# Expert rows of a mixture-of-experts kernel: loaded in 32x32 blocks and transposed by VectorE instead of TensorE

## Chip, cores and metric

One Trainium2 chip, 1 core. The metric is the device time of the whole program in microseconds (us); the median of three runs before the change is 1184.05 us.

## What is computed

The input x is (4, 1024, 256) in float32. The first layer adds to x the layernorm of a state-space mixer of layernorm(x). The second, which the change touches, adds the layernorm of a mixture of experts:

```python
xn = (xf - mu) * rsqrt(var + LN_EPS) * ln_gamma + ln_beta      # 4096 tokens x 256
topv, topi = top_k(softmax(xn @ router_w), 2)                   # 8 experts, 2 a token
for e in range(E):
    out = out + comb[:, e:e+1] * _swiglu(xn, gate_up_w[e], down_w[e])   # F = 1024
out = out + _swiglu(xn, shared_gate_up_w, shared_down_w)
```

_swiglu is silu(clip(gate)) * up @ down. All is done to float32 accuracy: each operand is split into a high and a low part, and a product is three matmuls (high x high, high x low, low x high).

## The kernel before

**Mixer stage** (to about 465 us of the profile). Four batches pass through the mixer, and each engine follows a list of stages written out by hand (ORDER, one string for each engine). Beside it, the experts' weights are split into high and low parts: SyncE loads chunk after chunk (`n0` to `n15` of each batch; `load_raw`, L385), ScalarE rounds it (L776) and VectorE subtracts (L1014), SyncE stores the two halves (L397, L398). A slot of the ring of three is loaded again once its stores have landed. Tokens are normalised (without gamma and beta), routed, and scattered by GpSimd (L1150) into `xs_scratch`, one row of ROW = 260 floats each: 256 values and four that hold token, expert code and shares. The shared expert runs there too.

**Expert stage** (488 to 1135 us, and its first group from 465 us). The rows lie sorted by expert and are taken in NG = 39 groups of G = 256 rows; a group belongs to one expert. The groups of the expert with most rows come first (`star`), so that its rows and weights can be loaded ahead: SyncE's stages `rw` (`first_rows`, L1253 to L1256, groups 0 and 1) and `ww` (`first_weights`). Each engine then runs `turn(g)` over the FC = 8 chunks f of the hidden width:

- TensorE: `gate_up(g, f)` is 12 matmuls (L1354 to L1356), `down` 6 (L1365 to L1367), LAG = 3 chunks behind, so that a turn's first three downs are the group before's chunks 5 to 7. After `gate_up` 1 and 4 it transposes one 128-column half c of the next group's rows into PSUM (`turn_rows`, L1342: two 128x128 transposes against `ident`).
- VectorE: clip of the gate (L1464), low part of the chunk before (`h_low`, L1459), product with the up part (L1471); after chunk 2 `weigh`, after 3 and 6 `rows_lo` (L1437), after 3 `copy_y` (L1443).
- ScalarE: `h_high` (L1406), silu (L1414), and after chunks 2 and 5 `rows_hi`: two activations with gamma and beta from the transposed rows in PSUM (L1397, L1400).
- SyncE: for each f, once `down` of the group before has used the chunk's buffers, two weight loads (L1239 the gate-up part, 512 KB; L1240 the down part, 256 KB) under a condition: they move data only where the expert changes, and `gate_up(g, f)` waits for both. After chunk 1 comes `load_rows(g+1)` (L1226, L1227): a register load of the row number, and one DMA of 256 x 1040 bytes. Before it SyncE waits for the last transposes (`x_turned`) and for `weigh`. `others` begins with group 2's rows (its first issue of L1227) and then walks the turns.
- GpSimd: two indirect DMAs a group that add the outputs to `acc_scratch` (L1304).

`gate_up(f)` needs VectorE's product of chunk f-2 (the semaphore `h_ready` starts at 2). Weights, rows and hidden parts live in parts of the mixer's buffers ("homes"); down parts 0 to 5 lie in one buffer behind the gate-up parts, except part 1, which lies in `h_hi[0]`; parts 6 and 7 lie behind a gate-up part in `xs_hi` and `xs_lo`, part 6 at offset 0 behind it. A last stage (1135 us on) normalises and adds x.

```python
if c == 0:
    pe.wait_ge(rows_loaded[par], (g_half(g, par)) * 16 + 16)
pe.wait_ge(x_f_ready, g * DC + c + 1)
for t in range(GT):
    i = nc.tensor.transpose(x_ps[:, t * P:(t + 1) * P], rows[:, par, t, c * P:(c + 1) * P], ident[:, :])
```

Of the kernel before, what the change touches and what calls it, by code (L numbers as in the profile page):

```python
# [6 lines left out]
I32 = mybir.dt.int32  # L7
ALU = mybir.AluOpType
# [48 lines left out]
X_AT, D_AT, R_AT = 48, 48, 0  # L57
GUW = 2 * 4 * P
XS = 5


def mixer(nc, x, w_e, w_s, weights, full, consts, shared, xs_dram, x1_dram, acc_dram, fill, vec, ident,
# [3 lines left out]
    with ExitStack() as ctx:  # L66
# [157 lines left out]
        homes = (gu_ring, d_ring, quad(u_flat[:, R_AT:R_AT + 2 * GT * ROW]), quad(x_home[0]), quad(x_home[1]),  # L224
                 u_flat[:, R_AT + 2 * GT * ROW:R_AT + 2 * GT * ROW + DC * G].rearrange("p (c g) -> p c g", g=G),
                 cv_flat[:, 0:4 * G].rearrange("p (i g) -> p i g", g=G),
                 h_home[0].rearrange("p (i g) -> p i g", g=G), h_home[1].rearrange("p (i g) -> p i g", g=G),
# [35 lines left out]
        def used(k):  # L263
# [195 lines left out]
        def _(pe):  # L459
            first_turn, all_groups = e_tensor(pe)  # L460
# [159 lines left out]
            def sh_down(k, f):  # L620
# [3 lines left out]
                for t in range(2):  # L624
                    toks = slice((2 * f + t) * P, (2 * f + t + 1) * P)
                    for c in range(SC):
# [5 lines left out]
                           "g": sh_gate, "y": sh_down, "x": first_turn})  # L632
# [162 lines left out]
        def _(dve):  # L795
            seeds, first_lo, all_groups = e_vector(dve)
# [254 lines left out]
            run("vector", {"x": first_lo, "star": fullest, "m": x_moments, "p": split_low, "k": bias_sum, "c": conv_sides, "r": xs_remainder, "dt": delta_unit, "da": da_unit,  # L1051
# [127 lines left out]
def experts(nc, ctx, w_s, xs_dram, acc_dram, x1_dram, out, group_expert, group_change, group_row, group_code, vec, ident, neg_half,  # L1179
# [9 lines left out]
    w_gu, w_d, rows, xg_hi, xg_lo, xg_f, gate, hg_hi, hg_lo, y, acc, x1, small = homes  # L1189
# [16 lines left out]
    gu_ps, down_ps, x_ps = banks[0:2], [banks[2:4], banks[4:6]], banks[6]  # L1206
    loaded = [sem(f"chunk_loaded{f}") for f in range(FC)]
    rows_loaded = [sem(f"x_rows_loaded{i}") for i in range(2)]
    x_turned, x_hi_ready, x_f_ready, x_lo_ready = sem("x_turned"), sem("x_hi_ready"), sem("x_f_ready"), sem("x_lo_ready")
# [3 lines left out]
    y_added = [sem(f"y_added{i}") for i in range(2)]  # L1213

# [9 lines left out]
    def sync(sp):  # L1224
        def load_rows(g, par):
            row = sp.value_load(group_row[0:1, bass.ds(g, 1)], min_val=0, max_val=SPARE)  # L1226
            sp.dma_start(rows[:, par, :, :], xs_dram[bass.ds(row, G), :].rearrange("(t p) d -> p t d", p=P)  # L1227
                         ).then_inc(rows_loaded[par], 16)
# [24 lines left out]
        def first_rows(b, par=0):  # L1253
            row = sp.value_load(star[0:1, 1 + par:2 + par], min_val=0, max_val=SPARE)
            sp.dma_start(rows[:, par, :, :], xs_dram[bass.ds(row, G), :].rearrange("(t p) d -> p t d", p=P)
                         ).then_inc(rows_loaded[par], 16)  # L1256
# [8 lines left out]
        def others():  # L1265
# [17 lines left out]
            for par in range(2):  # L1283
                sp.wait_ge(rows_loaded[par], 16 * (NG // 2 + 1))
# [48 lines left out]
    def tensor(pe):  # L1333
        def turn_rows(g, par, c):

            if c == 0:
                pe.wait_ge(rows_loaded[par], (g_half(g, par)) * 16 + 16)
                if isinstance(g, int) and g == 0:
                    free(pe, "x_ps")
            pe.wait_ge(x_f_ready, g * DC + c + 1)  # L1340
            for t in range(GT):
                i = nc.tensor.transpose(x_ps[:, t * P:(t + 1) * P], rows[:, par, t, c * P:(c + 1) * P], ident[:, :])  # L1342
            i.then_inc(x_turned, 1)

# [13 lines left out]
        def down(g, par, f):  # L1358
            pe.wait_ge(h_lo_ready, g * FC + f + 1)
            if f == 0:  # L1360
                pe.wait_ge(y_ready, g + 1)
            for t in range(GT):
                toks = slice(t * P, (t + 1) * P)
                out = down_ps[par][t][:, 0:D]
                nc.tensor.matmul(out, hg_hi[:, f % 4, toks], d_hi[f], start=f == 0, stop=False)  # L1365
                nc.tensor.matmul(out, hg_hi[:, f % 4, toks], d_lo[f], start=False, stop=False)  # L1366
                i = nc.tensor.matmul(out, hg_lo[:, f % 4, toks], d_hi[f], start=False, stop=f == FC - 1)  # L1367
# [24 lines left out]
        return first_turn, rest  # L1392

    def scalar(act):
        def rows_hi(g, par, c):
            act.wait_ge(x_turned, g * DC + c + 1)
            nc.scalar.activation(xg_hi[:, par, c, :], x_ps[:, 0:G], ACT.Identity,  # L1397
                                 bias=vec[:, V_BE + c:V_BE + c + 1],
                                 scale=vec[:, V_G + c:V_G + c + 1]).then_inc(x_hi_ready, 1)
            nc.scalar.activation(xg_f[:, c, :], x_ps[:, 0:G], ACT.Identity,  # L1400
# [3 lines left out]
        def h_high(g, f):  # L1404
            act.wait_ge(h_ready, g * FC + f + 1 + 2)
            nc.scalar.activation(hg_hi[:, f % 4, :], gate[:, f % 4, :], ACT.Copy).then_inc(h_hi_ready, 1)  # L1406
# [27 lines left out]
    def vector(dve):  # L1434
        def rows_lo(g, par, c):
# [146 lines left out]
```

## Time and profile before

| what | value |
|---|---|
| runs | 1182.93, 1184.05, 1185.82 us; median 1184.05 |
| the profiled execution's own time | 1178.42 us |
| its span | 1176.3 us |
| PE busy | 1082.7 us (92%) |
| DVE busy | 833.1 us (71%) |
| ACT busy | 655.2 us (56%) |
| POOL busy | 302.2 us (26%) |
| DMA moved | 191.72 MB, mean 163 GB/s |
| mean granted TensorE clock | 0.973 of 2.4 GHz |
| chain that ended last | PE 75%, DVE 8%, issue 4%, DMA 4%, POOL 3%, SyncE's queue 3%, ACT 3% |

Times are from the span's start. PE is TensorE (PEld its weight load), DVE VectorE, ACT ScalarE, POOL GpSimd, SP or SPq SyncE, whose issues count as its queue's. The span's times are of the one profiled execution, 0.5% below the median of the runs.

### The profile page before, as it was taken

Reading aid. Unit: us, or ns where it says so; the run is one execution under the profiler, and the core shown is the slowest. Engines: PE = TensorE matmul, PEld = TensorE weight load, DVE = VectorE, ACT = ScalarE, POOL = GpSimd, SP = SyncE. Lnnn points to the kernel's source line nnn. Section 1 sums busy time; section 2 is a strip of 40 time slices with the busy share of each in tenths; the row PEclk is TensorE's granted clock in tenths of the full one; section 3 lists DMA queues with packets and bytes.
Section 4 is the critical chain, followed back from the end, with each engine's and each line's share of the span. In section 5 each row is a group of like instructions: output and inputs, shape, how many; then the busy total and the mean of one; then the engine's idle time right before and its main releaser. Section 6 shows DMA issues by size and latency. Waiting matters only on the chain.

```text
span 1176.3 us, 24227 instructions
## 1 busy us (share of the span) xinstructions
PE 1082.7 (92%) x7492; PEld 961.2 (82%) x7492; DVE 833.1 (71%) x2113; ACT 655.2 (56%) x1325; POOL 302.2 (26%) x358
## 2 busy tenths in 40 slices
PE   4889999899979998899999999999999999999940
PEld 2665776677757666899999999999999999999940
DVE  5996899898877766566666666666666666666645
ACT  6778867778574364444544454544445444545425
POOL 1142032733441534012211221122122212211225
PEclk9999999999998999999999999999999999999985
DMA  8654776974663789523321236746922268212239
GB/s 304 208 213 172 251 231 210 318 240 145 223 229 140 247 284 320 195 59 64 72 56 35 36 86 210 222 130 192 379 67 36 60 208 250 36 19 35 36 81 222
DMA packets 122219, 191.72 MB, mean 163 GB/s; under 512 B 9792, under 2 KB 76864, under 8 KB 122176
## 3 DMA queue, kind: packets, MB, share of 16 engines
q1 hardware_dynamic: 105760, 170.38, 42.7%
q0 software_dynamic: 16416, 20.85, 10.5%
q8 instruction: 17, 0.28, 0.1%
q14 instruction: 26, 0.21, 0.1%
HBM read 295.62 MB, written 86.41 MB: 325 GB/s over the span
## 4 chain that ended last, share of the span: by engine, by line
PE 75%; DVE 8%; issue 4%; DMA 4%; POOL 3%; SPq 3%; ACT 3%; another core or an unknown queue 0%; ACTq 0%; DVEq 0%; POOLq 0%
PE bank L1354 11%; PE bank L1356 11%; PE bank L1355 11%; PE bank L470 10%; PE bank L1365 6%; PE bank L1367 6%; PE bank L1366 6%; PE bank L464 4%; PE bank L465 3%; PE bank L466 3%; POOL xs_scratch L1150 2%; PE bank L1342 1%; DMA w_both<-w_split 1%; DVE h L902 1%; DVE xr L1495 1%
## 5 line engine op out<-in xcount | busy, mean ns | idle before, releaser
L1304 POOL DMA_INDIRECT acc_scratch<-cv,ids x78 | 124.3, 1594 | 548.5 <-DVE cv L1443 508.4
L1464 DVE TENSOR_SCALAR cv<-bank 128x256 f32<-128x256 f32 x312 | 132.3, 424 | 185.3 <-PE bank L1356 185.3
L1354 PE MATMUL bank<-h_hi,w_both 128*128 128x256 f32 x936 | 260.3, 278 | 1.7 <-DVE cv L1471 1.2
L1355 PE MATMUL bank<-h_hi,w_both 128*128 128x256 f32 x936 | 259.6, 277 | 0.0
L1356 PE MATMUL bank<-h_hi,w_both 128*128 128x256 f32 x936 | 259.6, 277 | 0.0
L1414 ACT ACTIVATE cv<-cv 128x256 f32<-128x256 f32 x312 | 130.5, 418 | 225.5 <-DVE cv L1464 224.7
L1406 ACT ACTIVATE h_lo<-cv 128x256 fp32r<-128x256 f32 x312 | 130.0, 417 | 114.9 <-DVE cv L1471 113.4
L1354 PEld LDWEIGHTS bank<-h_hi,w_both 128*128 128x128 f32 x936 | 176.5, 189 | 3.1 <-issue 2.1
L1356 PEld LDWEIGHTS bank<-h_hi,w_both 128*128 128x128 f32 x936 | 176.4, 188 | 0.0
L1355 PEld LDWEIGHTS bank<-h_hi,w_both 128*128 128x128 f32 x936 | 176.4, 188 | 0.0
L1471 DVE TENSOR_TENSOR cv<-bank,cv 128x256 f32<-128x256 f32 x312 | 132.6, 425 | 47.6 <-ACT cv L1414 43.9
L1459 DVE TENSOR_TENSOR h_lo<-cv,h_lo 128x256 fp32r<-128x256 f32 x312 | 129.7, 416 | 0.8 <-ACT h_lo L1406 0.6
L464 PE MATMUL bank<-xs_hi,w_both 128*128 128x512 f32 x224 | 99.8, 445 | 22.3 <-DVE delta L852 9.1
L1365 PE MATMUL bank<-w_both,h_lo 128*128 128x256 f32 x390 | 107.7, 276 | 0.0
L1366 PE MATMUL bank<-w_both,h_lo 128*128 128x256 f32 x390 | 107.7, 276 | 0.0
L1367 PE MATMUL bank<-w_both,h_lo 128*128 128x256 f32 x390 | 107.7, 276 | 0.0
L466 PE MATMUL bank<-xs_hi,w_both 128*128 128x512 f32 x224 | 90.0, 402 | 0.0
L465 PE MATMUL bank<-xs_lo,w_both 128*128 128x512 f32 x224 | 89.8, 401 | 0.0
L1150 POOL DMA_INDIRECT xs_scratch<-n,slot_now x64 | 69.6, 1087 | 62.1 <-DVE slot_now L990 33.0
L464 PEld LDWEIGHTS bank<-xs_hi,w_both 128*128 128x128 f32 x224 | 43.9, 196 | 40.2 <-issue 14.6
L1133 POOL TENSOR_TENSOR h_lo<-h,h_hi 128x512 fp32r<-128x512 f32 x32 | 49.0, 1535 | 106.2 <-ACT h_hi L724 106.0
L1365 PEld LDWEIGHTS bank<-w_both,h_lo 128*128 128x128 f32 x390 | 73.2, 188 | 0.0
(233 smaller groups left out, 2558.2 us busy)
## 6 DMA issues: line engine op xcount, KB each, us to landing
w_both<-w_split SPq DMA_DIRECT2D x228, 512.0 KB
w_both<-w_split SPq DMA_DIRECT2D x190, 256.0 KB
e_raw<-w_e SPq DMA_DIRECT2D x64, 384.0 KB
w_split<-e_high SPq DMA_DIRECT2D x64, 384.0 KB
w_split<-e_raw SPq DMA_DIRECT2D x64, 384.0 KB
xs_hi<-w_split SPq DMA_DIRECT2D x38, 512.0 KB
xs_lo<-w_split SPq DMA_DIRECT2D x38, 512.0 KB
u<-xs_scratch SPq DMA_DIRECT2D x40, 260.0 KB, 3.2
```

What stands on the lines that cost most here:

```text
L464: nc.tensor.matmul(out, hi, x_hi, start=first, stop=False)
L1354: nc.tensor.matmul(out, gu_hi[f][:, cols], xg_hi[:, par, c, :], start=c == 0, stop=False)
L1355: nc.tensor.matmul(out, gu_hi[f][:, cols], xg_lo[:, par, c, :], start=False, stop=False)
L1356: i = nc.tensor.matmul(out, gu_lo[f][:, cols], xg_hi[:, par, c, :], start=False, stop=c == DC - 1)
L1365: nc.tensor.matmul(out, hg_hi[:, f % 4, toks], d_hi[f], start=f == 0, stop=False)
L1366: nc.tensor.matmul(out, hg_hi[:, f % 4, toks], d_lo[f], start=False, stop=False)
L1367: i = nc.tensor.matmul(out, hg_lo[:, f % 4, toks], d_hi[f], start=False, stop=f == FC - 1)
L1406: nc.scalar.activation(hg_hi[:, f % 4, :], gate[:, f % 4, :], ACT.Copy).then_inc(h_hi_ready, 1)
L1414: nc.scalar.activation(gate[:, f % 4, :], gate[:, f % 4, :], ACT.Silu).then_inc(silu_ready, 1)
L1459: nc.vector.tensor_tensor(hg_lo[:, f % 4, :], gate[:, f % 4, :], hg_hi[:, f % 4, :], ALU.subtract).then_inc(h_lo_ready, 1)
L1464: nc.vector.tensor_scalar(gate[:, f % 4, :], gu_ps[f % 2][:, 0:G], CLIP, -CLIP, ALU.min, ALU.max).then_inc(clipped, 1)
L1471: nc.vector.tensor_tensor(gate[:, f % 4, :], gu_ps[f % 2][:, G:2 * G], gate[:, f % 4, :], ALU.mult).then_inc(h_ready, 1)
```

## The change

The rows of a group are no longer loaded as 256 rows of 1040 bytes but in 32x32 blocks, placed so that VectorE's transpose, which turns each 32x32 block by itself, gives the whole transposed half. That takes, for each group, 8 DMAs of 32 partitions x 8 blocks x 128 bytes (4 quarters q of the partitions, 2 halves c) and a ninth for the four extra columns (256 pieces of 16 bytes), into a home of their own (`meta`). TensorE's transposes and their place in PSUM go; VectorE gets `turn_rows`, between `h_low` and the wait for silu in chunks 1 and 4, one instruction of 128x256 each. ScalarE's `rows_hi` reads SBUF in place of PSUM. In the mixer stage TensorE's `x0/3 x1/3` become VectorE's `turn0/3 turn1/3`, placed before `w13/3`. Down parts 1 and 6 get regular homes, and in the first group chunk 4's hidden part has a home apart (`level`).

```diff
-        d_ring += [v[:, GUW + at:GUW + at + 2 * D] for v, at in zip(xs_flat, (0, D_AT))]
-        d_ring[1] = flat(h_hi[0][:, :, :])[:, GUW + HALF // 8:GUW + HALF // 8 + 2 * D]
+        d_ring += [v[:, GUW + D_AT:GUW + D_AT + 2 * D] for v in xs_flat]
+        level_home = [flat(v[:, :, :])[:, 4 * G + D_AT:5 * G + D_AT] for v in h_lo]
...
-                "... g1/5 y0/4 g0/6 y1/4 d0.11/3 x0/3 g1/6 d1.7/3 x1/3 d1.8/3 ..."
+                "... g1/5 y0/4 g0/6 y1/4 d0.11/3 g1/6 d1.7/3 d1.8/3 ..."
-                "w13/3 d0.12/3 x0/3 w14/3 clip0/6 w15/3 ..."
+                "turn0/3 turn1/3 w13/3 d0.12/3 x0/3 w14/3 clip0/6 w15/3 ..."
...
+    def hidden(g, f):
+        if isinstance(g, int) and g == 0 and f == FC - 1 - LAG:
+            return level
+        return hg_hi[:, f % 4, :], hg_lo[:, f % 4, :]
...
+        def load_blocks(row, par):
+            source = xs_dram[bass.ds(row, G), :]
+            for q in range(QUADS):
+                for c in range(DC):
+                    at = c * P + q * BLK
+                    sp.dma_start(rows[q * BLK:(q + 1) * BLK, par, c, :, :],
+                                 source[:, at:at + BLK].rearrange("(t i) j -> i t j", i=BLK)).then_inc(rows_loaded[par], 16)
+            sp.dma_start(meta[:, par, :, :], source[:, D:ROW].rearrange("(t p) k -> p t k", p=P)).then_inc(rows_loaded[par], 16)
+
         def load_rows(g, par):
             row = sp.value_load(group_row[0:1, bass.ds(g, 1)], min_val=0, max_val=SPARE)
-            sp.dma_start(rows[:, par, :, :], xs_dram[bass.ds(row, G), :].rearrange("(t p) d -> p t d", p=P)
-                         ).then_inc(rows_loaded[par], 16)
+            load_blocks(row, par)
...
         def turn(g, par):      # tensor
             for f in range(FC):
                 gate_up(g, par, f)
-                if f in (1, 4):
-                    turn_rows(g + 1, 1 - par, (f - 1) // 3)
...
     def vector(dve):
+        def turn_rows(g, par, c):
+            if c == 0:
+                dve.wait_ge(rows_loaded[par], g_half(g, par) * (16 * LOADS) + 16 * LOADS)
+            if not (isinstance(g, int) and g == 0):
+                dve.wait_ge(x_f_ready, g * DC + c)
+            nc.vector.transpose(turned[:, c, :], rows[:, par, c, :, :].rearrange("p t j -> p (t j)")).then_inc(x_turned, 1)
...
                     h_low(g - 1, FC - 1)
+                if f in (1, 4):
+                    turn_rows(g + 1, 1 - par, (f - 1) // 3)
                 dve.wait_ge(silu_ready, g * FC + f + 1)
```

## Rows read from the trace of the kernel before

**Rows 1.** Page, part 1: busy time, share of the span, instructions.
```profile
PE 1082.7 (92%) x7492; PEld 961.2 (82%) x7492; DVE 833.1 (71%) x2113; ACT 655.2 (56%) x1325; POOL 302.2 (26%) x358
```

**Rows 2.** Windows view, one group of the expert stage. Columns: stretch, length, busy time by engine, PEclk, DMA share, GB/s.
```profile
505.00:522.00 17.00, 17.00 (x152) 17.00 (x151) 11.22 (x32) 8.41 (x21) 3.19 (x2) 1.00 0.30 63
```

**Rows 3.** Instructions of line 1342, 505 to 700 us: min/median/max ns, first and last start.
```profile
L1342 PE MATMUL bank<-ident,u x48: 272/272/273, 506.1 to 698.1; 128*128 128x128 f32 x48
```

**Rows 4.** Timeline of TensorE, two chunks. Columns: start, length, engine, line.
```profile
622.83 0.28 PE L1354 MATMUL bank<-h_hi,w_both 128*128 128x256 f32 x1
...
624.19 0.38 PE L1342 MATMUL bank<-ident,u 128*128 128x128 f32 x2
...
625.12 0.28 PE L1354 MATMUL bank<-h_hi,w_both 128*128 128x256 f32 x1
...
627.17 0.28 PE L1354 MATMUL bank<-h_hi,w_both 128*128 128x256 f32 x1
```

**Rows 5.** Timeline of VectorE beside them.
```profile
624.39 0.42 DVE L1464 TENSOR_SCALAR cv<-bank 128x256 f32<-128x256 f32 x1 [0.71 <-PE bank L1356]
624.73 0.41 DVE L1459 TENSOR_TENSOR h_lo<-cv,h_lo 128x256 fp32r<-128x256 f32 x1
625.30 0.42 DVE L1471 TENSOR_TENSOR cv<-bank,cv 128x256 f32<-128x256 f32 x1 [0.15 <-ACT cv L1414]
```

**Rows 6.** SyncE's rows load for that group, and line 1227 as a whole.
```profile
616.62 0.40 SPq L1227 DMA_DIRECT2D u<-xs_scratch  x1
...
L1227 SPq DMA_DIRECT2D u<-xs_scratch x38: 55/387/405, 484.8 to 1108.6; - x38
...
DMA to landing us min/median/max: 2.7/3.2/6.2
```

**Rows 7.** Timeline of SyncE in a group that takes new weights.
```profile
782.11 0.60 SPq L1239 DMA_DIRECT2D w_both<-w_split  x1
...
787.04 0.56 SPq L1239 DMA_DIRECT2D w_both<-w_split  x1
```

**Rows 8.** Chain in order of time, same group: start, length, what.
```profile
787.89 6.08 DMA w_both<-w_split
...
794.09 0.38 PE bank L1354
```

**Rows 9.** Windows view, same group (columns as in Rows 2).
```profile
781.90:783.30 1.40, 1.40 (x15) 1.40 (x14) 1.40 (x5) 0.38 (x1) 0.00 (x0) 1.00 0.00 0
...
788.00:790.00 2.00, 2.00 (x20) 2.00 (x20) 1.47 (x5) 0.84 (x2) 0.00 (x0) 1.00 1.07 317
```

**Rows 10.** Timeline of SyncE after the first groups' rows.
```profile
428.97 0.39 SPq L376 DMA_DIRECT2D x_scratch<-xr  x1
429.41 0.49 SPq L385 DMA_DIRECT2D e_raw<-w_e  x1
...
436.20 0.35 SPq L385 DMA_DIRECT2D e_raw<-w_e  x1
```

**Rows 11.** Timeline of ScalarE, the last two weight chunks rounded.
```profile
436.62 0.83 ACT L776 ACTIVATE e_high<-e_raw 128x768 fp32r<-128x768 f32 x1
...
441.29 0.83 ACT L776 ACTIVATE e_high<-e_raw 128x768 fp32r<-128x768 f32 x1
```

**Rows 12.** Timeline of SyncE, rows of group 2.
```profile
484.78 0.39 SPq L1227 DMA_DIRECT2D u<-xs_scratch  x1
```

**Rows 13.** Timeline of TensorE, its wait for those rows and chunk 3 after it.
```profile
487.62 0.43 PE L1342 MATMUL bank<-ident,u 128*128 128x128 f32 x2 [3.63 <-DMA u<-xs_scratch]
...
492.26 0.28 PE L1354 MATMUL bank<-h_hi,w_both 128*128 128x256 f32 x1
```

**Rows 14.** Windows view, the clock after two idle times (columns as in Rows 2).
```profile
488.40:491.80 3.40, 3.40 (x19) 3.40 (x18) 0.24 (x1) 0.00 (x0) 0.00 (x0) 0.50 0.05 18
...
61.10:63.30 2.20, 0.04 (x1) 0.05 (x1) 2.20 (x3) 1.18 (x3) 2.09 (x2) 1.00 0.57 176
63.30:66.70 3.40, 3.40 (x15) 2.78 (x16) 3.37 (x6) 1.02 (x2) 0.67 (x2) 1.00 0.58 233
```

More of the change, by code:

```diff
@@ L56 @@
 WS = 3
-X_AT, D_AT, R_AT = 48, 48, 0
+X_AT, D_AT = 48, 48
 GUW = 2 * 4 * P
+BLK = 32
 XS = 5
@@ L187, in free @@
         def free(engine, what):
-            if what == "x_ps":
-                engine.wait_ge(yn_ready, 2 * B + 1)
-            elif what == "gu_ps":
+            if what == "gu_ps":
                 engine.wait_ge(s_hid, 4 * B)
@@ L1188, in experts @@
     LAG = 3
-    w_gu, w_d, rows, xg_hi, xg_lo, xg_f, gate, hg_hi, hg_lo, y, acc, x1, small = homes
+    w_gu, w_d, rows, meta, turned, xg_hi, xg_lo, xg_f, gate, hg_hi, hg_lo, level, y, acc, x1, small = homes
     gu_hi, gu_lo = [part[:, 0:4 * P] for part in w_gu], [part[:, 4 * P:8 * P] for part in w_gu]
@@ L1254, in first_rows @@
             row = sp.value_load(star[0:1, 1 + par:2 + par], min_val=0, max_val=SPARE)
-            sp.dma_start(rows[:, par, :, :], xs_dram[bass.ds(row, G), :].rearrange("(t p) d -> p t d", p=P)
-                         ).then_inc(rows_loaded[par], 16)
+            load_blocks(row, par)
         def first_weights():
@@ L1333, in tensor @@
     def tensor(pe):
[L1334 to L1343, printed above, removed]
         def gate_up(g, par, f):
@@ L1364, in down @@
                 out = down_ps[par][t][:, 0:D]
-                nc.tensor.matmul(out, hg_hi[:, f % 4, toks], d_hi[f], start=f == 0, stop=False)
-                nc.tensor.matmul(out, hg_hi[:, f % 4, toks], d_lo[f], start=False, stop=False)
-                i = nc.tensor.matmul(out, hg_lo[:, f % 4, toks], d_hi[f], start=False, stop=f == FC - 1)
+                nc.tensor.matmul(out, part_hi[:, toks], d_hi[f], start=f == 0, stop=False)
+                nc.tensor.matmul(out, part_hi[:, toks], d_lo[f], start=False, stop=False)
+                i = nc.tensor.matmul(out, part_lo[:, toks], d_hi[f], start=False, stop=f == FC - 1)
             i.then_inc(down_done, 1)
@@ L1391, in rest @@
                 down(NG - 1, (NG - 1) % 2, f)
-        return first_turn, rest
+        return rest
     def scalar(act):
@@ L1405, in h_high @@
             act.wait_ge(h_ready, g * FC + f + 1 + 2)
-            nc.scalar.activation(hg_hi[:, f % 4, :], gate[:, f % 4, :], ACT.Copy).then_inc(h_hi_ready, 1)
+            nc.scalar.activation(hidden(g, f)[0], gate[:, f % 4, :], ACT.Copy).then_inc(h_hi_ready, 1)
         def turn(g, par):
@@ L1446, in weigh @@
         def weigh(g, par):
-            meta = lambda at: rows[:, par, :, at:at + 1].rearrange("p t k -> p (t k)")
-            dve.wait_ge(rows_loaded[par], g_half(g, par) * 16 + 16)
+            column = lambda at: meta[:, par, :, at - D:at - D + 1].rearrange("p t k -> p (t k)")
+            dve.wait_ge(rows_loaded[par], g_half(g, par) * (16 * LOADS) + 16 * LOADS)
             if not (isinstance(g, int) and g < 2):
                 dve.wait_ge(y_added[par], g_half(g, par) * 16 * GT)
-            nc.vector.scalar_tensor_tensor(out=part[:, :], in0=meta(CODE), scalar=group_code[:, bass.ds(g, 1)],
-                                           in1=meta(MORE), op0=ALU.is_equal, op1=ALU.mult).then_inc(meta_steps, 1)
-            nc.vector.tensor_copy(ids[:, par, :], meta(ID).bitcast(I32))
+            nc.vector.scalar_tensor_tensor(out=part[:, :], in0=column(CODE), scalar=group_code[:, bass.ds(g, 1)],
+                                           in1=column(MORE), op0=ALU.is_equal, op1=ALU.mult).then_inc(meta_steps, 1)
+            nc.vector.tensor_copy(ids[:, par, :], column(ID).bitcast(I32))
             dve.wait_ge(meta_steps, g + 1)
-            nc.vector.tensor_tensor(share[:, par, :], part[:, :], meta(SECOND), ALU.add).then_inc(meta_ready, 1)
+            nc.vector.tensor_tensor(share[:, par, :], part[:, :], column(SECOND), ALU.add).then_inc(meta_ready, 1)
         def h_low(g, f):
             dve.wait_ge(h_hi_ready, g * FC + f + 1)
-            nc.vector.tensor_tensor(hg_lo[:, f % 4, :], gate[:, f % 4, :], hg_hi[:, f % 4, :],
+            part_hi, part_lo = hidden(g, f)
+            nc.vector.tensor_tensor(part_lo, gate[:, f % 4, :], part_hi,
                                     ALU.subtract).then_inc(h_lo_ready, 1)
@@ L1516, in rest @@
             add_x1(NC - 1)
-        return seeds, first_lo, rest
+        return seeds, first_turn, first_lo, rest
     return sync, gpsimd, tensor, scalar, vector
```

32 lines of the change are left out of this document (19 added, 13 removed), and 4 rows, old and new, of the table ORDER.

## The prediction

> **What bounds the kernel.** I read the page first: TensorE is busy for 1082.7 us of the span [rows 1]. A stretch of the expert stage says where it counts: in 17.00 us, about one group, TensorE is busy throughout, VectorE for 11.22 us, and the DMA engines for 0.30 of the time [rows 2]. So there each us that TensorE is spared is a us of the span, VectorE has 5.8 us to spare, and DMA as bandwidth is no limit. What transposes cost must be read from starts, since a matmul's shown length overlaps the next. The chunk with a pair of transposes runs from 622.83 to 625.12, 2.29 us; the next, without, to 627.17, 2.05 us [rows 4]. That is 0.24 us a pair. Over 24 pairs from 506.1 to 698.1 [rows 3] lie 11 groups and 3 chunks, 91 chunks; at 2.05 us they take 186.6, so 5.4 us are left for 23 pairs, again 0.24; a chunk of 2.04 would give 0.28. I take 0.26.
>
> Then the resource on which the new work falls: SyncE. It issues the rows of the group under way at 616.62, and they are wanted at 624.19, with 3.2 us to landing in the median [rows 4, 6]. Where the expert changes it is another picture: SyncE's issue of chunk 2's down part at 787.89 lands 6.08 us later, and TensorE takes it 0.12 us after that [rows 8]. The weights set the pace there, without slack.
>
> **The change, part by part.**
>
> *Transposes off TensorE.* From the wait at 487.62 on there are 38 groups' pairs, 76 in all: 76 x 0.26 = 19.8 us less. The next thing TensorE meets is the next matmul, whose operands are there in an ordinary group. The moved homes of the down parts add no instruction; what they cost in the place after the transposes is inside the 2.29 us already, and I take nothing for them, nor for the one part of the first group.
>
> *Transposes on VectorE.* The trace has no VectorE transpose; the nearest rows are 128x256 operations of 0.41 to 0.42 us [rows 5]. Two a group are 0.8 us into 5.8 idle us. In chunk 1 it comes after 624.73 + 0.41 = 625.14, beside silu, and the product, which ran at 625.30, moves to about 625.55 and ends near 626.0; TensorE wants it for chunk 3 at 627.17, or 0.26 sooner [rows 4, 5]. So 0.9 us of cover; cost nothing, up to twice that length too. ScalarE's two activations only change their source; they are off the path.
>
> *Nine issues for one on SyncE.* A rows issue takes 0.387 us in the median [rows 6]. Two DMAs without registers follow at 428.97 and 429.41, 0.44 us apart [rows 10]; two weight loads with registers at 787.04 and 787.89, 0.85 apart with 0.54 to 0.56 of issue, so 0.29 beside it [rows 7, 8]. The bounds for one more issue are 0.44 and 0.85; I take 0.60, nearest to 0.39 + 0.29, since each new DMA takes its address from the row register as these do. Eight more are 4.8 us (3.5 to 6.8).
>
> In an ordinary group the ninth goes out at 616.62 + 4.8 = 621.4 and lands at 624.6; VectorE wants it at 625.1. Cover: 0.5 us and the 0.9 above. What is queued behind on SyncE are conditional weight issues that move nothing, and it has caught up before the turn ends. Cost nothing, by 1.4 us of cover.
>
> In a group with new weights, chunk 2's loads are queued behind the nine. They don't slip by all 4.8: data start 1.2 us after the first weight issue at 782.11 [rows 7, 9], and at 788 to 790 the DMA engines are full (share 1.07) [rows 9], so part of the 6.08 us is queueing. Into an empty queue 256 KB would land in about 3.9 us: 3.2 as the rows do [rows 6], and 0.7 behind the gate-up part. Queueing is 2.2, the slip 4.8 - 2.2 = 2.6 us, TensorE idle that long since its next chunk is late. Eight experts less the first make seven changes: 7 x 2.6 = 18.2. The transposes' gain between issue and use is lost in each (7 x 0.26 = 1.8): 20.0 us in all. Later chunks don't catch up, as DMA feeds them just at TensorE's pace. Bounds: 0 and 4.6 us a change, 0 to 34.
>
> *The first groups.* `rw` gets 16 more issues, 9.6 us, ahead of the raw-chunk load at 429.41 [rows 10], which goes to 439.0 and lands near 442.3; ScalarE rounded that chunk at 436.62 [rows 11]. The next, at 436.20, waits for stores that are 9.6 us later; with SyncE's waits giving some back I put it at 445, landing at 448.5, against ScalarE at 441.29 [rows 10, 11]: 7.2 us. Behind it, in order, ScalarE copies the tokens for the router, and behind the router lie plan, end rows and group 2's rows. With a little slack in TensorE's queue I take 6.5 us. Group 2's rows then start at 484.78 + 6.5 = 491.3 [rows 12], the ninth at 496.1, landing in 2.7 (the least) at 498.8; transpose and product take VectorE 0.8 more. TensorE waited 3.63 us for these rows, and reached chunk 3 at 492.26 [rows 13]. Now it runs to chunk 3, waits, and begins it at 499.7: 7.4 later. The clock: after the 3.63 us of idling it was at 0.50, the 1.2 GHz level, for 3.4 us [rows 14]; that is 1.7 us of work lost, already in 492.26, and lost again after 499.7. So 9.1 + 0.2 for `turn0`, `turn1` ahead of `w13`: 9.3 us (bounds 0 and 14).
>
> *The clock in the changes.* An idle time of 2.2 us leaves it at 1.00 [rows 14]; one of 3.63 is followed by half speed. Waits of 2.6 to 3 us lie between. I take one of seven, 1.7 us (bounds 0 and 12).
>
> **Sum:** -19.8 + 20.0 + 9.3 + 1.7 = +11.2 us. Against the profiled execution's own 1178.4 this is 1189.6. That execution is 0.5% below the median of the three runs, 1184.05, and the same difference on the median gives 1195.
>
> The Trainium skill, in "DMA: Bandwidth & Descriptors", section "Issuing engines are not separate DMA queues", says that a sequencer's time to start a DMA is usually small against the DMA. By that rule the eight issues would be nothing, and the sum -19.8, or 1164. For these blocks the rows speak against it: 32 KB in 0.39 us of issue.
>
> **Rivals.**
>
> *A, faster: SyncE is quick and the weights' queue swallows the rest.* Place: SyncE between chunk 1 and 2 of a change. At 0.44 an issue the slip is 3.5 - 2.2 = 1.3: 7 x 1.3 + 1.8 = 10.9 us; ahead of the stage 7.0 us are mostly taken up by SyncE's own waits, and 3.5 remain. -19.8 + 10.9 + 3.5 = -5.4: 1179. It decides at issues under 0.5 us. For it: the 0.44 spacing [rows 10]; against: registers. With the queue longer than I think, down to 1170.
>
> *B, the two cancel,* within 0.3% (3.6 us): issues of about 0.5 us, 1184.
>
> *C, rows late in every group.* With 0.85 an issue, or as much lost in landing, the ninth lands at 616.62 + 6.8 + 3.2 = 626.6; transpose and product end at 627.5, 0.6 after chunk 3 is due. 31 ordinary groups x 0.6 = 19, changes 34, start 14: -19.8 + 67 = +47, 1231. Against it: issue times of 0.39 [rows 6]. The trace's loads have no 128-byte pieces, so landing is open. The Trainium skill ("DMA: Bandwidth & Descriptors", "Rules for kernel authors") puts transfers under 64 KB down as mostly overhead; by that this case is the likely one.
>
> *D, nothing is saved,* because transposes hid under weight loads: rows 4 speak against it; no chance worth a share.
>
> **How the numbers follow.** The forecast has 0.57 (own range 1188 to 1210), A 0.20, B 0.13, C 0.10. A measurement can tell about 0.3% from no change. Faster 0.20, same 0.13, slower 0.57 + 0.10 = 0.67. The range goes from 1174, inside A, to 1216, leaving out the lower tail of A and most of C.
>
> **What the profile would show.** Right: no L1342; chunks of 2.04 us throughout and ordinary groups of about 16.3 us for 16.9; nine SyncE issues 0.6 us apart; TensorE waiting for w_split some 2.6 us at chunk 2 of seven groups; a wait of 6 us in group 1, behind VectorE's transpose; the stage beginning about 6 us later. Wrong: issues at 0.45, or chunk 2 landing as before (A); VectorE waiting for rows in ordinary groups (C); or a first stage that ends on time, which would take 6 us off.

## The result, and the profile after

| | before | after |
|---|---|---|
| median of the runs side by side | 1183.49 us (4 runs) | 1217.86 us (4 runs) |
| range | 1179.82 to 1185.82 | 1215.35 to 1223.69 |
| ratio | | 1.0302, 95% interval 1.0269 to 1.0336 |
| profiled execution, its span | 1178.42, 1176.3 | 1223.69, 1221.6 |

The change makes the kernel 34 us slower; 11 were forecast. The page of the kernel after: busy times, the chain by engine, and a group of the costliest list with the idle time ahead of it.

```profile
PE 1101.7 (90%) x7332; PEld 975.6 (80%) x7332; DVE 852.1 (70%) x2193; ACT 661.5 (54%) x1325; POOL 297.5 (24%) x358
...
PE 72%; DVE 7%; DMA 6%; SPq 6%; issue 5%; ACT 2%; POOL 1%; another core or an unknown queue 1%; ACTq 0%; DVEq 0%; POOLq 0%
...
L1360 PE MATMUL bank<-h_hi,w_both 128*128 128x256 f32 x936 | 266.3, 284 | 20.7 <-DMA w_both<-w_split 19.5
```

TensorE has 160 instructions fewer than in [rows 1] and is yet busy for 19 us more. By the windows view 12.7 us of these lie ahead of the expert stage, where it runs at half its clock for longer, and 6.2 in the stage: there its matmuls follow each other more slowly, which counts as busy. That they wait 19.5 us for weights is idle time and comes on top.

**An ordinary group** (one that keeps its expert's weights). Starts of chunks in the timeline of TensorE, first in the group of [rows 4]'s time, then in group 15 (groups are counted from 0).

```profile
617.74 0.28 PE L1360 MATMUL bank<-h_hi,xs_hi 128*128 128x256 f32 x1
...
619.86 0.28 PE L1360 MATMUL bank<-h_hi,xs_lo 128*128 128x256 f32 x1
...
621.98 0.28 PE L1360 MATMUL bank<-h_hi,w_both 128*128 128x256 f32 x1
...
743.98 0.28 PE L1360 MATMUL bank<-h_hi,w_both 128*128 128x256 f32 x1
...
746.02 0.28 PE L1360 MATMUL bank<-h_hi,w_both 128*128 128x256 f32 x1
```

A chunk takes 2.12 us in the first and 2.04 in the second, without a wait and at the full granted clock in both: 18 matmuls 117 to 119 ns apart, or 113 to 114. Eight chunks are 16.96 or 16.32 us. Before, with two pairs of transposes, a group took 16.86 us. Of the 29 ordinary groups among 2 to 37, only 15 and 20 are at 16.32; the 29 took 489.0 us before and take 490.6 now. The transposes' time has gone, and the matmuls have taken it.

**A group with new weights.** SyncE's timeline in group 19 (it begins at 815.50 on TensorE), and the chain there.

```profile
814.72 1.81 SPq L1240 DMA_DIRECT2D u<-xs_scratch  x4
816.72 0.39 SPq L1242 DMA_DIRECT2D st<-xs_scratch  x1
817.47 0.57 SPq L1257 DMA_DIRECT2D w_both<-w_split  x1
818.31 0.55 SPq L1258 DMA_DIRECT2D w_both<-w_split  x1
```

```profile
815.72 0.32 SPq L1240
...
816.22 0.32 SPq L1240
...
818.31 3.92 DMA w_both<-w_split
...
822.36 0.57 PE bank L1360
```

The rows' issues follow each other every 0.50 us, and the chain runs through them into chunk 2's down part, issued at 818.31. TensorE waits for that DMA. The view of its waits for the whole execution, and the windows around that wait and behind two others (columns as in [rows 2]):

```profile
PE bank L1360 <- DMA w_both<-w_split: 19.5, 11, 2.8
```

```profile
822.30:825.70 3.40, 3.35 (x16) 3.35 (x17) 0.38 (x2) 0.00 (x0) 0.00 (x0) 0.51 1.00 320
768.00:771.40 3.40, 3.40 (x19) 3.40 (x19) 1.50 (x6) 1.23 (x3) 0.00 (x0) 0.56 0.95 314
860.40:863.80 3.40, 3.40 (x20) 3.40 (x20) 1.55 (x6) 1.27 (x3) 0.00 (x0) 0.59 0.94 304
```

Seven of the eleven waits are at chunk 2 (16.0 us), three (0.9 to 1.1 us) at chunk 3, and one (0.5) at chunk 1 of group 22. Behind three of the seven the clock falls to its 1.2 GHz level for 3.4 us. The seven groups took 121.0 us before and take 146.5 now: 19.1 of these 25.5 us are the waits (before it waited 0.4), 5.1 the clock (half of three times 3.4).

**The start.** SyncE's timeline, the next-to-last issues that answer to [rows 10], and ScalarE's that answer to [rows 11].

```profile
436.37 3.89 SPq L1240 DMA_DIRECT2D u<-xs_scratch  x8
440.45 0.40 SPq L1242 DMA_DIRECT2D st<-xs_scratch  x1
441.62 3.83 SPq L1240 DMA_DIRECT2D u<-xs_scratch  x8
445.63 1.01 SPq L1242 DMA_DIRECT2D st<-xs_scratch  x1
...
447.21 0.50 SPq L387 DMA_DIRECT2D e_raw<-w_e  x1
...
453.58 0.35 SPq L387 DMA_DIRECT2D e_raw<-w_e  x1
```

```profile
451.62 0.84 ACT L778 ACTIVATE e_high<-e_raw 128x768 fp32r<-128x768 f32 x1 [3.14 <-DMA e_raw<-w_e]
453.35 0.76 ACT L764 ACTIVATE xnt<-bank,vec 128x512 f32<-128x512 f32 x1
458.16 0.84 ACT L778 ACTIVATE e_high<-e_raw 128x768 fp32r<-128x768 f32 x1 [4.04 <-DMA e_raw<-w_e]
458.90 0.76 ACT L764 ACTIVATE xnt<-bank,vec 128x512 f32<-128x512 f32 x1
```

The 18 issues take 10.3 us, the raw chunks come later, ScalarE waits 7.2 us for them, and the copy of the tokens for the router (L764) stands behind it. TensorE, whose matmuls for the router then wait 3.17 us, drops to half clock twice before the first group, at 460.4 and at 484.3 (windows view). Its last wait ahead of the stage is 3.01 us, where before the last three were of 0.78 each (the fence behind the windows).

```profile
484.00:487.60 3.60, 3.23 (x9) 2.63 (x9) 0.00 (x0) 0.23 (x1) 0.00 (x0) 0.54 1.05 400
460.40:467.20 6.80, 6.80 (x22) 5.57 (x22) 5.07 (x22) 4.10 (x8) 0.68 (x1) 0.50 1.01 381
```

```profile
484.37 3.60 PE L472 MATMUL bank<-w_sh,delta 128*128 128x256 f32 x8 [3.01 <-issue]
```

The first matmul of group 0 and, as a mark in the part that the change leaves alone, the one that 1350 others of TensorE precede; it ran at 363.74 before.

```profile
372.85 0.63 PE L468 MATMUL bank<-xs_hi,w_both 128*128 128x512 f32 x1
...
487.56 0.53 PE L1360 MATMUL bank<-h_hi,w_both 128*128 128x256 f32 x1
```

The stage begins at 487.6 instead of 464.6. Of these 23.0 us 9.1 are there at the mark already. Of the 13 profiles of this case that mark lies between 361.4 and 372.9, roughly by how often the clock fell ahead of it (mean granted clock up to the mark 0.95 here, 0.97 before, 0.98 at 361.4, in e5). The kernel before is at 363.7, and kernels with the same nine issues (e3, e7) at 361.5 and 362.5. It is chance of one execution, not the change. From the mark to the stage it was 100.9 us and is 114.7, so 13.8 more. How much of that is the change's is less sure: the other six profiles with nine loads ahead of the stage have 8.1 to 16.8 more, and four with five loads, the same up to the stage (e2, e5, e6, e9), 3.8 to 10.8.

**The sum of it**, from span to span: 9.1 chance, start 13.8, group 1 -5.35 (16.96 for 22.31, since the wait of [rows 13] is gone), ordinary groups +1.6, the changes +25.5, group 0 and the end +0.6: 45.3, as the spans differ. Without the 9.1 it is 36, beside 34 between the medians.

### The profile page after: what moved, and what is told of

It reads as the page before. It is cut to its first block, busy times and chain, and to the rows that moved or that the text cites. A ratio compares the mean times of both kernels' runs of the same rounds, so it can differ in the third digit from the quotient of the medians.

```text
span 1221.6 us, 24889 instructions
## 1 busy us (share of the span) xinstructions
PE 1101.7 (90%) x7332; PEld 975.6 (80%) x7332; DVE 852.1 (70%) x2193; ACT 661.5 (54%) x1325; POOL 297.5 (24%) x358
## 4 chain that ended last, share of the span: by engine, by line
PE 72%; DVE 7%; DMA 6%; SPq 6%; issue 5%; ACT 2%; POOL 1%; another core or an unknown queue 1%; ACTq 0%; DVEq 0%; POOLq 0%
PE bank L472 11%; PE bank L1360 11%; PE bank L1361 10%; PE bank L1362 10%; PE bank L1372 5%; PE bank L1373 5%; PE bank L1374 5%; PE bank L466 4%; PE bank L468 4%; PE bank L467 4%; DMA w_both<-w_split 3%; SPq L1240 2%; DMA w_split<-e_raw 1%; SPq L1257 1%; SPq L1258 1%
## 5 line engine op out<-in xcount | busy, mean ns | idle before, releaser
L1360 PE MATMUL bank<-h_hi,w_both 128*128 128x256 f32 x936 | 266.3, 284 | 20.7 <-DMA w_both<-w_split 19.5
L1362 PE MATMUL bank<-h_hi,w_both 128*128 128x256 f32 x936 | 263.9, 282 | 0.0
L1361 PE MATMUL bank<-h_hi,w_both 128*128 128x256 f32 x936 | 263.9, 282 | 0.0
L1321 POOL DMA_INDIRECT acc_scratch<-cv,ids x78 | 121.5, 1558 | 577.2 <-DVE cv L1452 533.5
L1360 PEld LDWEIGHTS bank<-h_hi,w_both 128*128 128x128 f32 x936 | 179.3, 192 | 24.1 <-issue 17.2
L1361 PEld LDWEIGHTS bank<-h_hi,w_both 128*128 128x128 f32 x936 | 178.2, 190 | 0.0
L1362 PEld LDWEIGHTS bank<-h_hi,w_both 128*128 128x128 f32 x936 | 177.7, 190 | 0.0
L1483 DVE TENSOR_TENSOR cv<-bank,cv 128x256 f32<-128x256 f32 x312 | 129.3, 415 | 36.0 <-ACT cv L1416 33.0
L1373 PE MATMUL bank<-w_both,h_lo 128*128 128x256 f32 x468 | 131.3, 280 | 0.0
L1372 PE MATMUL bank<-w_both,h_lo 128*128 128x256 f32 x468 | 131.2, 280 | 0.0
L1374 PE MATMUL bank<-w_both,h_lo 128*128 128x256 f32 x468 | 131.2, 280 | 0.0
L466 PE MATMUL bank<-xs_hi,w_both 128*128 128x512 f32 x224 | 102.1, 456 | 23.2 <-DVE delta L854 9.9
L468 PE MATMUL bank<-xs_hi,w_both 128*128 128x512 f32 x224 | 92.7, 414 | 0.0
L467 PE MATMUL bank<-xs_lo,w_both 128*128 128x512 f32 x224 | 92.3, 412 | 0.0
L1372 PEld LDWEIGHTS bank<-w_both,h_lo 128*128 128x128 f32 x468 | 88.9, 190 | 0.0
L1373 PEld LDWEIGHTS bank<-w_both,h_lo 128*128 128x128 f32 x468 | 88.3, 189 | 0.0
L1374 PEld LDWEIGHTS bank<-w_both,h_lo 128*128 128x128 f32 x468 | 88.1, 188 | 0.0
```

The costliest lines, as they stand in the source:

```text
L466: nc.tensor.matmul(out, hi, x_hi, start=first, stop=False)
L467: nc.tensor.matmul(out, hi, x_lo, start=False, stop=False)
L468: return nc.tensor.matmul(out, lo, x_hi, start=False, stop=last)
L1360: nc.tensor.matmul(out, gu_hi[f][:, cols], xg_hi[:, par, c, :], start=c == 0, stop=False)
L1361: nc.tensor.matmul(out, gu_hi[f][:, cols], xg_lo[:, par, c, :], start=False, stop=False)
L1362: i = nc.tensor.matmul(out, gu_lo[f][:, cols], xg_hi[:, par, c, :], start=False, stop=c == DC - 1)
```

## The experiments

Each was timed in turn with the kernel before, whose median on that chip is given. "Changes" is the sum of the seven groups with new weights (before 121.0, after 146.5), "start" the first matmul of group 0.

### e1: nine loads, transposes left on TensorE

```diff
 kernel before
-    sp.dma_start(rows[:, par, :, :], source)
+    for k in range(9):
+        cols = slice(k * 32, min(k * 32 + 32, ROW))
+        sp.dma_start(rows[:, par, :, cols], source[:, :, cols])
```

> This is the kernel before, with TensorE's transposes kept and only the load of a group's rows cut into nine DMAs of 256 pieces (128 bytes each, 16 in the ninth). Theory 1 (the slowdown is SyncE's issues plus a slower pace of TensorE's matmuls, which comes with the missing transposes): only the issues act, matmuls stay 113 ns apart, ordinary groups stay at 16.87 us, seven weight changes cost 3 to 4 us more each and the start about 5: 30 us over the kernel before, 1213. Theory 2 (the nine issues or their short pieces slow the matmuls themselves, as DMA traffic to SBUF beside them): ordinary groups go above 17.2 us too and the time is above 1220. Theory 3 (the issues cost little): within 5 us of the kernel before.

Measured 1219.89 us (1215.97 to 1224.56), before 1183.59; ratio 1.0308 (1.0255 to 1.0361). Changes 150.9, ordinary groups 16.86 as before. The loads alone bring the whole loss; moving the transposes takes nothing off it. Theory 1 had 1213.

### e2: four loads of 256-byte pieces, and one for the four meta columns

```diff
 kernel after
-            for q in range(QUADS):
-                for c in range(DC):
-                    at = c * P + q * BLK
-                    sp.dma_start(rows[q * BLK:(q + 1) * BLK, par, c, :, :], ...)
+            for q in range(QUADS):
+                at = q * DC * BLK
+                sp.dma_start(rows[q * BLK:(q + 1) * BLK, par, :, :], ...)
```

VectorE's transposes read with a stride; features, gate-up weights, gamma and beta are permuted to match.

> The changed kernel with five row DMAs a group in place of nine: a quarter of the partitions takes 256-byte pieces that hold both halves, with the experts' weights and gamma and beta laid out to match. Theory 1 (issues on SyncE, some 0.52 us each, set what a weight change costs): four fewer issues take 2.1 us off each of seven changes and 4 us off the start: 15 to 18 us under the changed kernel, about 1201; ordinary groups stay at 16.96. Theory 2 (the data of many short pieces, not the issues): the same bytes in pieces twice as long, a gain of 5 us or less.

Measured 1187.65 us (1178.54 to 1194.98), before 1183.59; ratio 1.0049 (1.0003 to 1.0095). Start 471.5, changes 130.1. Four issues fewer take 30 us off, twice what theory 1 gave them (1201): by the profiles 16.4 us in the changes, 5.7 from the mark to the stage, and 3.2 in ordinary groups, which stay at 16.96 up to group 29 and run at 16.32 from 31 on. The pieces are also twice as long here, so this run alone doesn't part issues from pieces; e10 does.

### e3 and e4: idle transposes on TensorE

```diff
 kernel after, e3
             for f in range(FC):
                 gate_up(g, par, f)
+                if f in (1, 4):
+                    for t in range(GT):
+                        nc.tensor.transpose(banks[6][:, t * P:(t + 1) * P], ident[:, :], ident[:, :])
```

e4 has one such transpose a group, after chunk 1.

> The changed kernel, and TensorE transposes the identity twice after gate_up 1 and 4 into an unused bank: the work the change removed, without its waits and read by nobody. Theory 1 (matmuls run 113 or 118 ns apart by the state the pipeline is in, and a pair of transposes brings back the 113): ordinary groups go from 16.96 to 16.87 us although 0.5 us of work is added, and the time stays within 3 us of the changed kernel. Theory 2 (the 118 comes from where operands lie in SBUF, or from VectorE's or the DMAs' traffic): ordinary groups take 17.5 us, and the time is 17 to 20 us over the changed kernel.

> As the kernel with dummy pairs, but one identity transpose a group only, after gate_up 1. Theory 1 (the pace is a state that any disturbance resets): ordinary groups 16.32 + 0.15 = 16.5 us, that is 0.45 under the changed kernel's in 31 of them, 14 us off the changed kernel's time, about 1204. Theory 2 (pace set by placement or traffic): ordinary groups 17.1 us, 5 us over the changed kernel. If it takes a pair, or two a turn, to reset: also 17.1.

e3: 1215.49 us (1213.91 to 1220.73), ratio 1.0293 (1.024 to 1.0345); e4: 1217.27 (1213.17 to 1218.57), ratio 1.0285 (1.0237 to 1.0334). In e3 groups with four instructions more take 16.83 us, less than the 16.96 without, as theory 1 had it; the rival that placement or traffic sets the pace (17.5 us) is out. In e4 groups 1 to 13 take 16.60 and 16.94 in turn, not the 16.5 of theory 1, and the 14 us that it was to gain are not there. The timeline of e4 in groups 5 and 6:

```profile
566.12 0.28 PE L1362 MATMUL bank<-h_hi,w_both 128*128 128x256 f32 x1
...
568.24 0.28 PE L1362 MATMUL bank<-h_hi,w_both 128*128 128x256 f32 x1
...
582.72 0.28 PE L1362 MATMUL bank<-h_hi,w_both 128*128 128x256 f32 x1
...
584.76 0.28 PE L1362 MATMUL bank<-h_hi,w_both 128*128 128x256 f32 x1
...
586.12 0.27 PE L1383 MATMUL bank<-ident 128*128 128x128 f32 x1
...
586.94 0.28 PE L1362 MATMUL bank<-h_hi,w_both 128*128 128x256 f32 x1
587.29 0.28 PE L1362 MATMUL bank<-h_hi,w_both 128*128 128x256 f32 x1
```

A chunk of 2.12 us (566.12 to 568.24); after that group's transpose chunks of 2.04 (582.72 to 584.76); after the next one the matmuls of L1362 are 0.35 us apart again (586.94 to 587.29) where they were 0.34. In groups 1 to 13 one transpose turns the pace over, either way, each time, and the pace stays until the next. Behind changes it doesn't always: in groups 18, 24, 27, 32 and 35 (17.07 us) the transpose leaves the slower pace as it was.

### e5 and e7: a pair after chunk 1 only, and pairs in the first group only

e5 is the kernel of e2 with e3's pair after chunk 1 alone; e7 the changed kernel with both pairs in group 0 alone (`if g == 0 and f in (1, 4)`).

> The kernel with four row loads, plus two TensorE transposes of the identity into an unused bank after chunk 1's gate-up in every group: two small operations of extra work a group (about 0.24 us) that nothing reads. Theory 1 (a transpose between the chunks returns TensorE's matmuls to their quicker pace, 113 ns apart, and what disturbed it is not undone otherwise): ordinary groups go from 16.96 to about 16.6 us, start and changes stay as with four loads (471.5 and 130), so 1187.7 - 11 = about 1176, faster than before. Rival (pace has another source, transposes only cost): 1187.7 + 38 x 0.24 = 1197.

> The changed kernel with pairs of idle TensorE transposes after gate-up 1 and 4 in the very first group only. Theory 1 (TensorE has two paces of matmuls, 113 and 118 ns, and keeps the one it is in until a wait or a transpose disturbs it): groups 2 to 13 run at 16.32 us instead of 16.96, until the first group with new weights, so about 8 us less than 1217.9, 1210. Rival (the quicker pace needs a transpose in every group): groups 2 to 13 at 16.96, time 1218. Second rival (128-byte pieces of the rows slow TensorE's reads): 16.96 as well.

e5: 1186.61 us (1175.18 to 1194.56), before 1181.4, ratio 1.0029 (0.9998 to 1.0059). Groups 2 to 13 take 17.18 us: the pair costs 0.22 and leaves the pace at 2.12 a chunk. From group 25 on they take 16.57. So theory 1 in its form "a pair restores the quicker pace" falls, and with it its 1176. e7: 1210.67 us (1202.37 to 1211.96), ratio 1.0234 (1.0186 to 1.0282); groups 2 to 13 at 16.96, as the rivals had it, though not for their reason. Its timeline at the end of group 0 and the start of group 1:

```profile
491.82 0.28 PE L1362 MATMUL bank<-h_hi,xs_hi 128*128 128x256 f32 x1
...
493.87 0.28 PE L1362 MATMUL bank<-h_hi,xs_lo 128*128 128x256 f32 x1
...
495.94 0.28 PE L1362 MATMUL bank<-h_hi,w_both 128*128 128x256 f32 x1
...
498.06 0.28 PE L1362 MATMUL bank<-h_hi,w_both 128*128 128x256 f32 x1
```

Group 0 ends at the quicker pace (2.05), its last chunk has six matmuls 120 ns apart (2.07), and group 1 runs at 2.12. Group 1 is the first turn inside the loop over the groups, and each profile of a kernel built on the changed one that comes to that place at the quicker pace leaves it at the slower (e2, e3, e4, e7, e8, e9), with a pair in group 0 or without. The kernel before and those built on it (e1, e10, e11) pass the place at the quicker pace; why was not found. That e7 is 7 us faster than the changed kernel all the same is mostly the quicker pace that it falls into behind changes (groups 17, 18, 20 and 31 to 37 at 16.32; 5.1 us less over the ordinary groups); the rest is not explained.

The kernel before shows what it had by its transposes. Group 30 there, a change:

```profile
984.14 0.28 PE L1354 MATMUL bank<-h_hi,w_both 128*128 128x256 f32 x1
986.26 0.28 PE L1354 MATMUL bank<-h_hi,w_both 128*128 128x256 f32 x1
...
987.68 0.38 PE L1342 MATMUL bank<-ident,u 128*128 128x128 f32 x2
988.61 0.29 PE L1354 MATMUL bank<-h_hi,w_both 128*128 128x256 f32 x1
990.67 0.28 PE L1354 MATMUL bank<-h_hi,xs_hi 128*128 128x256 f32 x1
992.71 0.28 PE L1354 MATMUL bank<-h_hi,xs_lo 128*128 128x256 f32 x1
```

A short wait left it at 2.12 a chunk, and the pair after chunk 4 brought it back to 2.06 and 2.04. With two pairs a group (before, e1, e3, e10, e11) every ordinary group from 2 on is at the quicker pace, but for one chunk or two of one group of e3; with one pair it depends.

### e6: rows issued by ScalarE

```diff
 kernel of e2, scalar's turn, for the rows of groups 3 to 38
+                if f >= 3:
+                    load_block(act, row, par, f - 3)     # blocks 0 to 3, then the meta columns
 sync's turn
-                if f == 1:
-                    load_rows(g + 1, 1 - par)
```

> The kernel with four row loads, the five row issues of groups 3 to 38 moved from SyncE to ScalarE, one in each of chunks 3 to 7, so that no row issue stands between the weight issues of chunks 1 and 2. Theory 1 (what SyncE issues ahead of chunk 2's weights sets the changes): the seven change groups together fall from 130 us to 121 or less (before's 121 has one row issue there), so about 1177 to 1179. Rival (the pieces themselves load the DMA queues, whoever issues them): the changes stay at 130 and the time at 1188. Third: issues hold ScalarE up in front of its silu, and ordinary groups go over 17 us.

Measured 1185.69 us (1176.1 to 1192.95), before 1181.4; ratio 1.0038 (1.0008 to 1.0068). Changes 127.1, hardly less than e2's 130.1, with TensorE still waiting 6.4 us for weights, seven times. Neither the theory's 121 nor quite the rival's 130. With no row issue on SyncE 0.9 us a change is left over e11's 121.1, below. SyncE's lateness is not what is left. In group 21, which begins at 829.51, chunk 2's down part is issued 2.7 us ahead of that start, where before (group 19) it was 1.5 ahead, and TensorE waits for it all the same (chain in order of time):

```profile
826.84 7.70 DMA w_both<-w_split
...
834.66 0.38 PE bank L1360
```

It takes 7.70 us to land, for 6.08 in [rows 8]. So here the time is in the transfers themselves; which of them hold it up was not found. Of e2's 9.1 us over before, 3.0 went with SyncE's issues and 6.0 stayed.

### e8: the rows' loads later in the order ahead of the stage

```diff
 kernel of e2, ORDER
-sync    "... n11/3 rw/3 st1/3 n12/3 sh/3 n13/3 n14/3 n15/3 ..."
+sync    "... n11/3 st1/3 n12/3 sh/3 n13/3 n14/3 rw/3 n15/3 ..."
```

VectorE's `turn0/3 turn1/3` and the steps on them are moved back likewise.

> The kernel with four row loads, with the first two groups' row loads moved three places back in SyncE's order ahead of the stage, behind the load of the last raw chunk, and VectorE's two first transposes and the activations on them moved back likewise. Theory 1 (the row issues ahead of the stage hold up the raw chunks that the router waits for, and that moves the stage): the stage begins at 465 to 468 us instead of 471.5, and the time falls by 4 to 6 us, to about 1183. Rival (the start is moved by clock drops in the part before, not by the order of the issues): start at 471 and time at 1188.

Measured 1192.18 us (1188.65 to 1201.13), before 1181.4; ratio 1.0108 (1.0068 to 1.0148), and the start at 481.0, 116.5 us from the mark where e2 has 109.0. Both theories missed (465 to 468, and 471). In this one trial the later place was the worse one; why was not followed up.

### e9: e6 with a pair, after chunk 1 and chunk 4 in turn

> The kernel with four row loads issued from ScalarE's queue, with one pair of idle TensorE transposes a group, after chunk 1 in one group and after chunk 4 in the next. The runs before showed that TensorE keeps one of two paces, that the entry of the loop over the groups leaves it in the slower one, and that a pair never ends the quicker one and ends the slower one only at some points of its pattern. Theory: two places give two points, so that one of them ends the slower pace within a few groups: ordinary groups at 16.57 us from group 4 or so on, instead of 17.18, which saves about 10 x 0.4 = 4 us before the first change and as much behind it against 1185.7, so 1178 to 1182, within 0.3% of before. Rival: both places fall on points that leave it, ordinary groups at 17.18 and 1190.

Measured 1186.61 us (1179.12 to 1191.16), before 1180.41; ratio 1.0051 (1.0023 to 1.008). The rival came: groups 1 to 13 at 17.18, and from the first change on mostly 16.57. No kernel of this study beats the one before.

### e10: nine loads of whole rows

The eight-fold pieces and the nine issues were together in e1. This cuts the load by partitions instead.

```diff
 kernel of e1
-            for k in range(LOADS):
-                cols = slice(k * 32, min(k * 32 + 32, ROW))
-                sp.dma_start(rows[:, par, :, cols], source[:, :, cols])
+            cuts = [16 * k for k in range(8)] + [120, P]
+            for a, b in zip(cuts, cuts[1:]):
+                sp.dma_start(rows[a:b, par, :, :], source[a:b, :, :])
```

> The kernel before, transposes on TensorE as they were, its one row load cut into nine by partitions, so that SyncE issues nine DMAs while the pieces stay whole rows of 1040 bytes and their number stays as before. Theory (the nine issues themselves make the cost): as with nine loads of 32 columns, the seven change groups at about 150 us and the stage beginning late, 1215 to 1220. Rival (the eight-fold number of 128-byte pieces makes it): the changes stay at 121 to 125 us and the time at 1184 to 1190. Between the two, each has its share.

Measured 1214.64 us (1205.94 to 1215.65), before 1180.41; ratio 1.0273 (1.0219 to 1.0328). Changes 145.9; 115.9 us from the mark to the stage; group 1 16.85. The line of the waits for weights in e10, and the same of e2 and e11:

```profile
PE bank L1359 <- DMA w_both<-w_split: 17.9, 15, 2.5
```

```profile
PE bank L1360 <- DMA w_both<-w_split: 5.5, 9, 1.6
```

```profile
PE bank L1360 <- DMA w_both<-w_split: 0.2, 1, 0.2
```

So the nine loads make the cost, not the short pieces. In the changes of e10 SyncE issues chunk 2's down part 2.4 to 3.0 us behind the start of the group, of the kernel before 1.3 to 1.8 ahead of it. Of e1's 29.8 us in the changes e10 has 24.9. The 4.9 between them are not shown to be the pieces': in e1 the clock fell five times in the changes, for 3.4 us each, which costs 8.5 us, in e10 never, and the intervals of the two ratios overlap. By its profile e10 loses 15.0 at the start, 24.9 in the changes and gains 5.5 in group 1: 34.4; it measured 34.2.

### e11: nine loads for the first two groups only

The kernel before, with e10's nine loads in `first_rows` alone and one load for every later group.

> The kernel before with only the row loads of the first two groups (those issued ahead of the stage) cut into nine by partitions, whole rows as pieces; every later group's rows come by one DMA as before. It measures the start's share by itself. The profiles of nine loads have the stage beginning about 14 to 16 us later, counted from TensorE's matmul 1350, than before. Theory (that delay is the 16 more issues ahead of the raw chunks): start about 14 us later, group 1 no longer than 17.5 us instead of 22.3, since the wait for group 2's rows is passed in the delay, the seven changes at 121, so 1180.4 + 14 - 5 = about 1190. Rival (the later start in the profiles is the clock in the unchanged part before it): start at 101 us behind matmul 1350 as before, 1181. Second rival (group 1 keeps its 22.3 us because the rows' own load sets it): 1195.

Measured 1179.49 us (1177.57 to 1184.01), before 1169.43 on this chip; ratio 1.0085 (1.0051 to 1.0118), 10 us. Changes 121.1, group 1 17.72; from the mark to the stage 109.0, that is 8.1 more than before, where the six other profiles with nine loads ahead of the stage have 13.8 to 16.8 more (after, e1, e3, e4, e7 and e10). Up to there e10 has the same instructions and takes 6.9 us longer. The clock makes little of it: it falls to half speed for 10.2 us in e11 (at 442 and 452) and for 11.2 in e10 (at 446, 453 and 480). More of it are two waits of TensorE in e10, 1.69 us at 473.3 and 4.13 at 479.4, where e11 has 0.78 each; their cause was not traced. The theory's 10 us came, but its parts (14 and -5) did not: in the profile they are 8.1 and -4.6, 3.5 together. The profile of the kernel before is not from this chip, on which its median is 14 us lower, and the other 6.5 us are not explained. What the start costs by itself is thus known to some us only.

## Why the prediction was wrong

**The step that failed** is "Transposes off TensorE: 76 x 0.26 = 19.8 us less", with the sentence "The next thing TensorE meets is the next matmul". The price of a pair was right: in e3 and e5 a pair costs 0.22 to 0.26 us. What was wrong is that the rest of the chunk was taken as fixed at 2.04. Without transposes TensorE mostly runs at a second pace of 2.12, 0.64 us a group, and 2 pairs at 0.25 to 0.27 are 0.5 to 0.54. The forecast groups of 16.3 us are there, twice in 29. The 29 ordinary groups were to save 29 x 2 x 0.26 = 15.1 us and cost 1.6: 16.7 of the 24 us by which the forecast falls short of the profile. The rival that nothing is saved had the right size for a wrong reason, and it was given no chance. The rows that the forecast used show one pace only, but the trace of the kernel before holds the other too (group 30, at e7 above).

**The seven changes, 20.0 + 1.7.** Mechanism and place were right: the rows' issues push chunk 2's weights back, and TensorE waits there 7 times. In group 19 chunk 2's down part was issued 1.5 us ahead of the group's start and is issued 2.8 behind it, 4.3 later for the 4.8 forecast: an issue takes 0.50 us, not 0.60, so that eight of them are 4.0; the other 0.3 was not traced. It lands 3.92 us behind its issue (forecast 3.9) for 6.08, so the queue swallows the 2.2 us that it was to swallow. The waits sum to 19.1 against 20.0 forecast, though three of them are at chunk 3 and one at chunk 1. The clock fell in three of seven, not one: 5.1 for 1.7. Together 24.2 for 21.7; with 3.6 us of these groups' transposes taken off, 20.6 for 18.1. Measured are 25.5: the other 4.9 are matmuls that follow each other more slowly between the waits.

**The first groups, 9.3.** The wait for raw chunks was right: 7.2 us forecast and 7.2 (3.14 + 4.04) found. But the 6.5 made of it became 13.8: two drops of the clock before the stage, not in the sum, cost 5.0 us (the kernel before has none from 366 us on), and the wait of 3.01 us in place of 0.78 another 2.2. And the lengthened wait for group 2's rows didn't come: these rows were issued late by as much as their user was, and the wait went instead (-5.35). 13.8 - 5.35 is 8.5, beside 9.3: luck, by two errors of opposite sign.

**Nothing in ordinary groups for VectorE and the rows.** Right. Each VectorE transpose takes 0.44 us, and it waited 0.2 us in all for them (view by line):

```profile
L1442 DVE STREAM_TRANSPOSE u<-u x80: 404/438/447, 446.1 to 1168.3; 128x256 f32<-128x256 f32 x80
```

Rival C is out: 32 KB blocks landed in 2.3 us in the median, less than the 3.2 of the whole load. The Trainium skill ("DMA: Bandwidth & Descriptors", "Rules for kernel authors") says that a transfer under 64 KB pays mostly overhead; the trace agrees as far as an eighth of the bytes took 2.3 us for 3.2, but no wait in ordinary groups came of it. Rival A needed issues under 0.5 us, and a wait of 1.3 us a change; issues are at 0.50, and the waits at chunk 2 are 2.3 in the mean. Rival B had the size of an issue right (about 0.5 us) and put the time at 1184, since it too took the transposes as gained. The range, up to 1216, was 2 us short: its upper end took in dear issues, but no loss of the gain.

The Trainium skill ("DMA: Bandwidth & Descriptors", "Issuing engines are not separate DMA queues") has the time to start a DMA as usually small against the DMA. Here it was 0.50 us against 2.3, and nine times that ahead of the weights cost most of the loss: e10 moves the same rows in the same pieces as before and loses 34 us.

**The sum again**, with the transposes put where they were: ordinary groups -15.1 became +1.6, changes +18.1 became +25.5, first groups 9.3 - 1.0 = 8.3 became 8.4 (group 0 with it). Forecast 11.3, found 35.5 by the profile and 34 by the medians.

## What to carry to other kernels

Count DMA issues on the queue that feeds the bottleneck: cutting one load into nine cost 34 us here (e10) without moving a byte more, in the seven places where the weights behind it had no slack, and at the start. Moving the issues to another queue gave back only part of it (e6), for a reason that was not found. Work taken off the bounding engine is only gained if what remains keeps its pace: read the interval between its instructions in more than one stretch, behind stalls too, before a duration is multiplied by a count. And a late start moves both a load and its user: a wait is lengthened only by the difference.

## What the hardware showed unasked

The same stream of matmuls (128x128 by 256 columns, full granted clock, no wait) runs at 113 to 114 ns or at 117 to 119 ns from one to the next, and keeps either for a hundred matmuls and more. A wait of 0.2 us, one transpose, or the entry of a loop turned it from one to the other, none of them every time; a pair of transposes never ended the quicker one in an ordinary group and ended the slower one only at some places. What sets it inside TensorE stays open. And one execution's time in an unchanged first part of 365 us differs by 11 us, roughly by how often the clock falls there, which is as much as the whole forecast difference: a span is compared with a span only from a common mark on.
